# Two depthwise convolutions as Toeplitz products: the middle product of the 31x31 one is split once more, and the outer additions stay in PSUM

## The reference, cut to what matters

```python
# x: (32, 192, 56, 56) float32; _gn is a group normalisation, 32 groups of 6 channels, over 6 x 56 x 56 values
x = x + conv(_gn(x), L0_conv_weight) + L0_conv_bias_term   # depthwise 31x31, one filter per channel, padding 15
x = x + conv(_gn(x), kernels)                              # depthwise 11x11, filters made from 4 points per channel, padding 5
```

## Time and profile before

| | us |
|---|---|
| median of 3 runs | 3654.97 (3654.81 to 3655.27) |
| the profiled execution | 3656.55 |
| its span | 3654.5 |
| TensorE busy | 3546.5 (97%) |
| VectorE busy | 3028.6 (83%) |
| ScalarE busy | 1181.4 (32%) |
| GpSimd busy | 904.1 (25%) |
| share of the 16 DMA engines, main queue | 74.4% |

### The profile page before, as it was taken

How to read it: one execution, slowest core, us unless ns; L and a number is a source line. 1 busy time by engine, 2 the same in 40 slices (tenths; PEclk the granted TensorE clock), 3 DMA queues, 4 the chain that set the end, 5 groups by cost and what they waited for, 6 DMA issues and landing times.

```text
span 3654.5 us, 60386 instructions
## 1 busy us (share of the span) xinstructions
PE 3546.5 (97%) x19008; PEld 3336.8 (91%) x19008; DVE 3028.6 (83%) x4451; ACT 1181.4 (32%) x1250; POOL 904.1 (25%) x480
## 2 busy tenths in 40 slices
PE   5899999999999999999999999999999999999997
PEld 5799999999999999999999999999999999999996
DVE  6788888888888888888888888888888888888877
ACT  3233333333333333333333333333333333333332
POOL 6112222222222222222222222222222222222222
PEclk9999999999999999999999999999999999999999
DMA  9977777777767777777877677787678776778653
GB/s 187 187 142 150 147 150 140 147 156 158 144 136 142 157 146 151 150 136 146 159 155 147 138 142 157 145 153 149 133 144 159 155 150 140 145 152 157 116 116 85
DMA packets 810125, 536.20 MB, mean 147 GB/s; under 512 B 464808, under 2 KB 772136, under 8 KB 809576
## 3 DMA queue, kind: packets, MB, share of 16 engines
q1 hardware_dynamic: 809416, 534.36, 74.4%
q10 hardware_dynamic: 544, 0.38, 0.1%
HBM read 449.06 MB, written 85.48 MB: 146 GB/s over the span
## 4 chain that ended last, share of the span: by engine, by line
PE 74%; DVE 12%; issue 9%; SPq 1%; POOL 1%; ACT 0%; DVEq 0%; DMA 0%; POOLq 0%
PE acc L1069 74%; DVE x_lo L875 3%; DVE y_image L895 2%; DVE yt L885 2%; DVE part L852 1%; POOL xt L633 1%; SPq L440 1%; DVE raw L903 1%; DVE halves L814 1%; DVE norm L845 0%; DVE xt L861 0%; DVE agg L809 0%; DVE halves_tmp L821 0%; SPq L450 0%; ACT small L682 0%
## 5 line engine op out<-in xcount | busy, mean ns | idle before, releaser
L1069 PE MATMUL acc<-x_hi,toep 128*112 128x448 f32 (+3 forms) x12672 | 3389.9, 348 | 101.1 <-DVE x_lo L875 72.7
L1069 PEld LDWEIGHTS acc<-x_hi,toep 128*112 128x112 f32 x12672 | 2261.0, 181 | 246.5 <-issue 94.7
L1069 PE MATMUL acc<-x_lo,toep 128*112 128x448 f32 (+3 forms) x6336 | 2208.9, 349 | 0.0
L633 POOL TENSOR_TENSOR xt<-xt 128x960 f32<-128x960 f32 x368 | 832.8, 2263 | 2668.4 <-DVE xt L861 2668.4
L1069 PEld LDWEIGHTS acc<-x_lo,toep 128*112 128x112 f32 x6336 | 1142.5, 180 | 63.9
L665 ACT ACTIVATE x_hi<-xt 128x1440 fp32r<-128x1440 f32 x384 | 540.9, 1409 | 1739.8 <-POOL xt L633 1657.1
L885 DVE TENSOR_TENSOR yt<-acc,p 128x896 f32<-128x896 f32 x384 | 414.7, 1080 | 490.2 <-PE acc L1069 329.7
L875 DVE TENSOR_TENSOR x_lo<-xt,x_hi 128x1440 fp32r<-128x1440 f32 x384 | 630.4, 1642 | 10.6 <-ACT x_hi L665 10.6
L861 DVE STREAM_TRANSPOSE xt<-images 128x960 f32<-128x960 f32 x384 | 447.4, 1165 | 18.3 <-ACT images L657 1.3
L657 ACT ACTIVATE images<-raw,norm 128x896 f32 (+1 forms) x384 | 439.1, 1144 | 26.3 <-DVE norm L845 26.3
L852 DVE BATCH_NORM_STATS2 part<-raw 96x6 f32 (+3 forms) x768 | 444.6, 608 | 1.3
(11 more groups left out here) (55 smaller groups left out, 244.4 us busy)
## 6 DMA issues: line engine op xcount, KB each, us to landing
toep<-padded SPq DMA_DIRECT2D x384, 276.0 KB
toep<-padded SPq DMA_DIRECT2D x384, 234.0 KB
toep<-padded SPq DMA_DIRECT2D x384, 186.0 KB
out_dram<-raw SPq DMA_DIRECT2D x189, 336.0 KB, 5.0
raw<-in_x_dram SPq DMA_DIRECT2D x93, 672.0 KB, 10.4
toep<-padded SPq DMA_DIRECT2D x768, 58.5 KB
toep<-padded SPq DMA_DIRECT2D x384, 69.0 KB
toep<-padded SPq DMA_DIRECT2D x384, 47.2 KB
```

The source lines that it names most:

```text
L633: nc.gpsimd.tensor_tensor(differences_held(), *(sequences if PATTERN[s][0] == FIRST else sequences[::-1]), ALU.subtract).then_inc(xd_ready, 1)
L1069: last = nc.tensor.matmul(dst, toeplitz(toep, f, place, part, k), src[:, h, cols], start=(m == matrices[0][0] and part == 0 and src is x_h ...
```

## The change

Four things change.

1. **The middle product of filter 1 is split again.** Its sequence of 14 pairs is split in halves of 7 in the same way (three products of 4 matrices for one of 8 on twice the columns): `products` now gives five for filter 1, three narrow ones of 224 or 192 columns (12 matrices, 36 matmuls) and the two outer ones as before (48 matmuls). The narrow ones need a second difference on GpSimd (`differences_of_halves`, 512 values), a larger operand (1728 values in two pieces in `high` and `low`), sums of sums of the filters (28 matrices for 24, so larger Toeplitz blocks, padded filters and DMAs) and one more addition on VectorE, `combine`.
2. **The outer additions are written in place in PSUM.** `outputs` writes to `acc`, `transpose_out` reads it and writes `yt` in SBUF, `add_residual` reads `yt`; `y_image` is gone, and `acc` gets a fourth bank. TensorE waits for `transpose_out` of two jobs before ahead of its outer products.
3. **The operand buffers** become two places for FIRST jobs and one for SECOND jobs; `high` of a SECOND job now waits for the end of the SECOND job before it.
4. **Moves.** The first part of the normalisation's chain (aggregates and copies) stands ahead of `transpose_in`, the statistics of slot 0 go from slot 2 to slot 4, the next group's statistics are spread otherwise, stage 2 of the filters is stored later and in parts, and several small tiles and `w1_later` lie in space that is free at the start.

```diff
-MEASURED = {0: [0], 1: [1], 4: [2, 3], 6: [4, 5]}
+MEASURED = {0: [0, 1], 1: [2], 4: [3], 6: [4, 5]}
...
+        first_sum, first_halved = self.D, self.D + self.D // 2
+        pairs_of_taps = range(self.halved)
         return [
-            (*b, [(m, self.D + m) for m in taps]),
-            (*d1, [(m, 2 * m) for m in taps]),
-            (*d3, [(m, 2 * m + 1) for m in taps]),
+            (0, 0, 2 * JE + 2 * JZ, -1, JZ, JQ, [(n, first_halved + n) for n in pairs_of_taps]),
+            (3, 0, 2 * JE, -1, JZ, JQ, [(n, first_sum + 2 * n) for n in pairs_of_taps]),
+            (3, JQ, 2 * JE + JZ, -1, JZ, JQ, [(n, first_sum + 2 * n + 1) for n in pairs_of_taps]),
+            (1, 0, 0, -3, JE, JH, [(m, 2 * m) for m in taps]),
+            (2, 0, JE, -3, JE, JH, [(m, 2 * m + 1) for m in taps]),
         ]
...
                 if k == 5:
-                    store_filters(2, 0, CP // 3)
-                if k == 6:
-                    store_filters(2, CP // 3, CP)
-                if k == 7:
-                    filters_stored()
+                    store_filters(2, units=[0])
+                if k == 8:
+                    sp.wait_ge(w_lo_ready, 2 * BEFORE[3])
                     sp.wait_ge(x_landed, 16 * BANDS)
                     load_x(2)
+                    store_filters(2, 0, CP // 2, units=[1])
+                if k == 9:
+                    store_filters(2, CP // 2, CP, units=[1])
...
+                if PATTERN[s][0] == FIRST:
+                    nc.gpsimd.tensor_tensor(differences_held(), shifted_even(), repeated_odd(), ALU.subtract)
+                    nc.gpsimd.tensor_tensor(*differences_of_halves(), ALU.subtract).then_inc(xd_ready, 1)
...
             def low(i, s):
...
-                nc.vector.tensor_tensor(x_lo[:, h, :], operand(s), x_hi[:, h, :].bitcast(F32), ALU.subtract
-                                        ).then_inc(lo_ready, 1)
...
+                for source, low_part, high_part in parts[:-1]:
+                    nc.vector.tensor_tensor(low_part, source, high_part.bitcast(F32), ALU.subtract)
+                source, low_part, high_part = parts[-1]
+                nc.vector.tensor_tensor(low_part, source, high_part.bitcast(F32), ALU.subtract).then_inc(lo_ready, 1)
+
+            def combine(i, s):
+
+                f = first_ordinal(i, s)
+                dve.wait_ge(p2_copied, job(i, s) + 1)
+                dve.wait_ge(u_done, f + 1)
+                nc.vector.tensor_tensor(p2_by_parity(), sums_view(i, s), p2_common(), ALU.add).then_inc(comb_ready, 1)
...
-                nc.vector.tensor_tensor(yt[:].rearrange("p (s n) -> p s n", s=2),
-                                        acc[:, ring(i, s, P_RING), 1:3, 0:JH * B],
-                                        p2[:].unsqueeze(1).to_broadcast([P, 2, JH * B]), ALU.add).then_inc(y_ready, 1)
+                nc.vector.tensor_tensor(outer(i, s), outer(i, s), p2[:].unsqueeze(1).to_broadcast([P, 2, JH * B]),
+                                        ALU.add).then_inc(y_ready, 1)
...
-                nc.vector.tensor_tensor(rows, y_image[:, 0:N].rearrange("p (j h e) -> p h j e", h=HB, e=2), rows, ALU.add
+                nc.vector.tensor_tensor(rows, yt[:].rearrange("p (j h e) -> p h j e", h=HB, e=2), rows, ALU.add
                                         ).then_inc(residual_added, 1)
...
-                    after_norm2 = s == 2 and len(slots(i)) == SLOTS
+                    after_norm2 = s == 4 and len(slots(i)) == SLOTS
+                    early2 = s == 2 and group2 is not None
+                    early1 = s == NORM1_SLOT and measure_next and len(slots(i)) == SLOTS
...
+                    if early2:
+                        normalisation_begins(norm2_ordinal(group2), group2, part2, parts2_ready)
+                    if early1:
+                        normalisation_begins(i * 2 + 1, i + 1, part1, parts1_ready)
                     if after:
                         transpose_in(*after)
...
+                        combine(i, s)
...
+                    if k == before_outer and positive(n + 1 - P_RING):
+                        pe.wait_ge(image_ready, n + 1 - P_RING)
```

More of the change, by code:

```diff
@@ L154, in ring, with first_ordinal, place, place_free @@
     return job(i if isinstance(i, int) else 2, s) % size
+def first_ordinal(i, s):
+    return i * CG + PATTERN[s][1]
+LAST_SHORT = 8
+def place(i, s):
+    if isinstance(i, int) and i >= GROUPS:
+        return PLACES[(job(i, s) - (GROUPS * SLOTS - LAST_SHORT)) % 3]
+    return PLACES[PATTERN[s][1] % F_PLACES] if PATTERN[s][0] == FIRST else PLACES[F_PLACES]
+def place_free(i, s):
+    if isinstance(i, int) and i >= GROUPS:
+        return job(i, s) - 2
+    conv, n = PATTERN[s][0], job(i, s)
+    if conv == FIRST:
+        if isinstance(i, int) and i < 2:
+            firsts = [(a, b) for a in range(2) for b in slots(a) if PATTERN[b][0] == FIRST]
+            at = firsts.index((i, s)) - F_PLACES
+            return job(*firsts[at]) + 1 if at >= 0 else 0
+        return n - 3
+    return n - 1
 def later(i, s, k):
@@ L330, in conv_norm_kernel, with sums_done @@
         BEFORE = [0, 2, 6, 8]
+        def sums_done(k, u):
+            units = [f for stage in STAGES for f, _, _ in stage][:BEFORE[k] + u + 1]
+            return sum(f.sum_steps for f in units)
         def scratch(k, u):
             f = STAGES[k][0][0]
-            return WORK_START[k] + (u % WORKS[k]) * (f.K * 3 * f.D)
+            return WORK_START[k] + (u % WORKS[k]) * (f.K * 2 * (f.D + f.sums))
         def work(k, u):
@@ L369, in untapped @@
             return places
-        BUFS_ZEROED = 1 + 2 * I_RING + sum(len(margins(0, u)) + len(untapped(0, u)) for u in range(len(STAGES[0])))
+        BUFS_ZEROED = 3 + 2 * I_RING + sum(len(margins(0, u)) + len(untapped(0, u)) for u in range(len(STAGES[0])))
         def pairs(tile):
@@ L662, in high @@
                 act.wait_ge(xd_ready, n + 1)
[L663 to L665 removed]
+                free = place_free(i, s)
+                if positive(free):
+                    act.wait_ge(conv_done, free)
+                parts = operand_parts(i, s, x_hi)
+                for source, high_part in parts[:-1]:
+                    nc.scalar.activation(high_part, source, ACT.Copy)
+                source, high_part = parts[-1]
+                nc.scalar.activation(high_part, source, ACT.Copy).then_inc(hi_ready, 1)
             def copy_p2(i, s):
@@ L754, in filter_share @@
                     lay_taps(2, 1)
+                if n == 6:
                     high_taps(2, 1)
@@ L894, in transpose_out @@
                     dve.wait_ge(residual_added, n)
-                nc.vector.transpose(y_image[:, 0:N].rearrange("p (i s b) -> p s i b", s=2, b=B), pairs(yt[:])).then_inc(image_ready, 1)
+                nc.vector.transpose(yt[:].rearrange("p (i s b) -> p s i b", s=2, b=B),
+                                    outer(i, s).rearrange("p s (i b) -> p s i b", b=B)).then_inc(image_ready, 1)
             def add_residual(i, s):
@@ L1053, in toeplitz, with convolve @@
                 return bass.AP(toep, place * f.block + k * f.slab + part, [[T_RING * f.block, P], [2, M]])
-            def convolve(i, s, f, toep, place):
-                n, h, p = job(i, s), ring(i, s, H_RING), ring(i, s, P_RING)
-                done = {0: p2_done, 2: conv_done}
-                for bank, (start, shift, held, matrices) in enumerate(f.products()):
+            def convolve(i, s, f, toep, place_of_toep):
+                n, at, p = job(i, s), place(i, s), ring(i, s, P_RING)
+                done = [p2_done, None, u_done, None, conv_done] if f.halved else [p2_done, None, conv_done]
+                before_outer = 3 if f.halved else 1
+                for k, (bank, column, start, shift, held, count, matrices) in enumerate(f.products()):
+                    if k == before_outer and positive(n + 1 - P_RING):
+                        pe.wait_ge(image_ready, n + 1 - P_RING)
```

219 lines of the change are left out of this document (143 added, 76 removed).

## The result

The changed kernel takes **3795.55 us** (median; 3793.75 to 3796.36), the kernel before 3655.12 beside it: a ratio of 1.0383, 95% interval 1.0365 to 1.0401. The change makes the kernel 3.8% slower. The forecast was 3669, the range 3585 to 3740.

What follows compares the result with a forecast made beforehand. TensorE bounds the kernel, with two VectorE stretches per group level with it. Group: 111.43 - 4 x 0.72 (shorter matmuls) + 3.65 (longer stretches) = 112.2 us; 3655 + 23 (groups) - 9 (start and end) = 3669 us, range 3585 to 3740.

Steps and rivals of the forecast that it cites:

- the half clock behind it: Rival for TensorE's two pauses per looped group: each followed by half clock, +1.5 x 2 x 30, 3759 us; chance 0.08.

Runs made afterwards that it cites:

- the version at 3585.6 us: Changed kernel with each normalisation chain in three pieces in different slots, next group's statistics in slots 0, 2 and 4: 3585.6 us, 0.9808 of the kernel before.
- the run at 3734 us: The version at 3585.6 us with the low part ahead of `transpose_out` and the second convolution's residual addition behind the next transposition: 3734.4 us, 1.0216 of the kernel before.
- k = 3 and 4: Kernel before with three or four more statistics instructions (results unused) on VectorE in slot 2 of every looped group: 3717.7 and 3753.8 us.

## What to carry to other kernels

When a change takes work from the busiest engine, look where another engine's stretch runs level with it: there the saving turns into a pause, and the remedy is to spread that stretch over the places where its engine already waits, as the version at 3585.6 us does. Price a pause of TensorE of some 2 us or more with the half clock behind it, 1.5 us each, and put that case into the range; in a steady loop the group's length can make it fall behind nearly all such pauses or few of them. Count a path over several engines as a latency of its own: if it is the limit, filling its waits with other work keeps them free of cost, and emptying them, as the run at 3734 us did, brings the pauses back.

## What the runs showed of the hardware

- A fall of the clock behind a pause is recorded as a stretch of 3.4 us at the half clock and costs 1.51 to 1.57 us, whether the kernel is the changed one or the one before. In the kernel before with k = 3 and 4 the six that began 0.64 us or more ahead of the restart lasted 6.8 us.
- The instants at which the granted clock changes lie on an even grid in each trace. Whether a pause of a given length is followed by a fall was decided, in every looped pause of these runs from 1.82 us up, by where an instant of the grid lies against the restart.
- With idle matmuls of 64 columns in the two waits the clock stayed at 1.00 behind all but 4 of them, and a group took 3.03 us less. The 4 falls came behind rests of 0.65 us, 28 of them, though in the kernel before none of 28 pauses of 1.18 us had one; why isn't shown.
- A VectorE step of 32 partitions with seven values (2.12 us for 0.22) ends only with GpSimd's 2.26 us subtraction, and VectorE's addition of two SBUF tiles can hold GpSimd's likewise (3.02 us for 2.26).
- With a weight load of 112 columns for each, matmuls of 192 and 224 columns start 0.105 us apart alike. The first distance behind a pause is 0.1 us longer than usual (0.30 us for 0.20 at 448 columns, 0.20 for 0.105 at 224).
